# Bit-linear feed-forward: the scale and shift of the second norm computed by VectorE instead of GpSimd

## The chip, the core and the metric

The kernel runs on one core of a Trainium2 chip. Its time is the device time of one execution in microseconds, the median of several runs. Engines are named as the profile names them: PE is TensorE (PEld its weight loads), DVE is VectorE, ACT is ScalarE, POOL is GpSimd, SP is SyncE.

## What is computed

The program is a stack of four attention blocks, each followed by a feed-forward block, over 64 x 64 tokens of width 128 (`x`, kept in SBUF for the whole run). The change touches the first feed-forward block alone, whose reference is:

```python
def layernorm(x, g, b):
    mu = jnp.mean(x, axis=-1, keepdims=True)
    var = jnp.mean((x - mu) ** 2, axis=-1, keepdims=True)
    return (x - mu) * jax.lax.rsqrt(var + LN_EPS) * g + b
def act_quant_fake(x):
    scale = 127.0 / jnp.clip(jnp.max(jnp.abs(x), axis=-1, keepdims=True), 1e-05)
    return jnp.clip(jnp.round(x * scale), -128.0, 127.0) / scale
def bitlinear(x, w, b):
    dqx = act_quant_fake(x)
    dqw = weight_quant_fake(w)
    return jnp.einsum('btd,hd->bth', dqx, dqw) + b
h = layernorm(x, ln1_g, ln1_b)
h = bitlinear(h, w1, b1)                  # 128 -> 512
h = jax.nn.gelu(h, approximate=False)
h = layernorm(h, ln2_g, ln2_b)            # the second norm, over 512
h = bitlinear(h, w2, b2)                  # 512 -> 128
```

`ln2_g` and `ln2_b` are rows of 512 values, the same for every token.

## The kernel before, in words

The 4096 tokens lie as 32 tiles of 128 tokens: partition = token within the tile, free axis = channel. `bit_ffn` (from L905) holds the block. Its first half runs over groups of four tiles and leaves the output of the gelu in `H`, 32 tiles of 128 x 512 float32 in SBUF, and its statistics in `stats`. Then VectorE works out mean, reciprocal deviation and shift of all tokens (L1029 to L1035).

The second half, which the change touches, runs over 16 pairs of tiles. A pair `k` goes through these steps, each on the engine named:

- ACT `normalise` (L1114): writes `(H - mean) * rstd` of the two tiles to slot `k % 4` of `hn` (four slots of 128 x 1024 float32), two ACTIVATE of 128 x 512 (L1117), and raises `n_ready`. It runs two pairs ahead.
- POOL `affine` (L1082): waits for `n_ready`, multiplies the slot by `g2` (L1086), adds `b2n` (L1088), both in place, and raises `affined` after each. `g2` and `b2n` are 128 x 512 tiles that hold the row in every partition; they are read twice through a broadcast access pattern.
- DVE `quantise_h` (L1039): waits for `affined`, then the largest absolute value per token (L1045), its limit and scale (L1046 to L1048, 2 elements per partition each), scaling of either tile (L1049, L1050), and clipping and rounding of both (L1051), which raises `rounded`.
- ACT `to_integers` (L1121) converts to bf16, PE `turn_h` (L1160) transposes eight 128 x 128 blocks, ACT `take_h` (L1126) copies them from PSUM to SBUF, PE `down` (L1167) does the eight matmuls.
- DVE `residual` (L1053): two SCALAR_TENSOR_TENSOR that read PSUM (L1057) and a TENSOR_TENSOR of 128 x 256 that adds to `X` (L1061). DVE `measure_x` (L1063): two BN_STATS for the next block's norm (L1066).

The order on each engine is written out by hand through `pipelined`: a list of (lead, stage), run in that order at each step, unrolled in fours, with a hardware loop in the middle. For VectorE it is

```python
pipelined(dve, PAIRS, [(-2, residual), (0, quantise_h), (-3, measure_x)], period=4)
```

so step `k` is `residual(k - 2)`, `quantise_h(k)`, `measure_x(k - 3)`; ScalarE does `take_h(k - 1)`, `normalise(k + 2)`, `to_integers(k)`. Operations of one engine that depend on each other are joined by `Chain.link` (L62): the instruction raises a semaphore and the engine waits for it. `B_LINKS` is the number of such links in one `quantise_h`. No DMA takes part in this half.

Of the kernel before, what the change touches and what calls it, by code (L numbers as in the profile page):

```python
# [13 lines left out]
ALU = mybir.AluOpType  # L14
# [7 lines left out]
P = 128  # L22
# [56 lines left out]
def wait_past(eng, sem, value):  # L79

    if not isinstance(value, int) or value > 0:
        eng.wait_ge(sem, value)
# [10 lines left out]
def peeled(eng, end, step):  # L93

    step(0, 0, 0)
    step(1, 1, 0)
    in_pairs(eng, 2, end, step)


def pipelined(eng, units, stages, period=2):  # L100

    stages = [(lead, stage, *(more or (0,))) for lead, stage, *more in stages]
    leads = [lead for lead, _, _ in stages]
    first = -(-(period - min(leads)) // period) * period
    end = (units - max(leads)) // period * period  # L110
    def plain(start, stop):
        for s in range(start, stop):
            for lead, stage, beyond in stages:
                if 0 <= s + lead < units + beyond:
                    stage(s + lead, (s + lead) % period, (s + lead) // period)

    if first >= end:
        plain(-max(leads), units - min(leads))
        return
    plain(-max(leads), first)  # L120
    with eng.Fori(0, (end - first) // period) as k:
        for s in range(first, first + period):
            for lead, stage, _ in stages:
                stage(period * k + (s + lead), (s + lead) % period, k + (s + lead) // period)
    plain(end, units - min(leads))
# [776 lines left out]
HID0 = 512  # L902


def bit_ffn(nc, m, t):  # L905
# [5 lines left out]
    with ExitStack() as own:  # L911
        def sb(name, shape, dt=F32):
            return own.enter_context(nc.sbuf_tensor(f"bit_{name}", shape, dt))
# [10 lines left out]
        b1, g2, b2n = sb("b1", [P, HID0]), sb("g2", [P, HID0]), sb("b2n", [P, HID0])  # L924
# [6 lines left out]
        hn = sb("hn", [P, 4, 2, HID0])  # L931
# [5 lines left out]
        def loads(sp):  # L937
# [14 lines left out]
            "xq_ready", "xq_turned", "xqT_ready", "up_ready", "biased", "gelued"))  # L952
        n_ready, hq_ready, hq_turned, hqT_ready, down_ready, x_added = (m.sem(n) for n in (
            "n_ready", "hq_ready", "hq_turned", "hqT_ready", "down_ready", "x_added"))
        affined, rounded, xn_ready, x_affined = m.sem("affined"), m.sem("rounded"), m.sem("xn_ready"), m.sem("x_affined")
        PAIRS = NT // 2
        LOADS = 16 * 8

        with nc.Block() as block:
            @block.vector  # L960
            def _(dve):
# [67 lines left out]
                c = Chain(dve, chained, before + A_LINKS * G)  # L1029
# [4 lines left out]
                c.link(dve.scalar_tensor_tensor(shift2[:, :], mean2[:, :], -1.0, rstd2[:, :], ALU.mult, ALU.mult))  # L1034
                dve.memset(y[:, 0, 0:1], 0.0).then_inc(r_in, 1)  # L1035
                before_b = c.base + c.n
                B_LINKS = 5

                def quantise_h(k, s, n):  # L1039

                    dve.wait_ge(affined, 2 * k + 2)
                    wait_past(dve, rounded, k)
                    c = Chain(dve, chained, before_b + B_LINKS * k)
                    h = hn[:, s, :, :]
                    c.link(dve.tensor_reduce(top2[:, :], h, AX.X, ALU.max, apply_absolute_value=True))  # L1045
                    c.link(dve.tensor_scalar(top2[:, :], top2[:, :], EPS, 1.0 / 127.0, ALU.max, ALU.mult))  # L1046
                    dve.tensor_scalar(undo2[:, s, :], top2[:, :], wmean[:, 1:2], None, ALU.mult)
                    c.link(dve.reciprocal(scale2[:, :], top2[:, :]))  # L1048
                    c.link(dve.tensor_scalar(hn[:, s, 0, :], hn[:, s, 0, :], scale2[:, 0:1], 127.0, ALU.mult, ALU.min))  # L1049
                    c.link(dve.tensor_scalar(hn[:, s, 1, :], hn[:, s, 1, :], scale2[:, 1:2], 127.0, ALU.mult, ALU.min))  # L1050
                    dve.tensor_scalar(h, h, -128.0, MAGIC, ALU.max, ALU.add).then_inc(rounded, 1)  # L1051
# [11 lines left out]
                def measure_x(k, s, n):  # L1063
                    dve.wait_ge(x_added, 2 * k + 2)
                    for j in range(2):
                        dve.bn_stats(m.stats[:, 2 * k + j, :], m.X[:, 2 * k + j, :])  # L1066

                pipelined(dve, PAIRS, [(-2, residual), (0, quantise_h), (-3, measure_x)], period=4)

            @block.gpsimd  # L1070
            def _(pool):
                def affine_x(g, u, n):

                    row = lambda v: v[:, :].unsqueeze(1).broadcast_to([P, 4, D])
                    pool.wait_ge(xn_ready, g + 1)
                    pool.tensor_tensor(xh[:, u, :, :], xh[:, u, :, :], row(g1), ALU.mult).then_inc(x_affined, 1)
                    pool.wait_ge(x_affined, 2 * g + 1)
                    pool.tensor_tensor(xh[:, u, :, :], xh[:, u, :, :], row(b1n), ALU.add).then_inc(x_affined, 1)

                peeled(pool, G, affine_x)  # L1080

                def affine(k, s, n):  # L1082

                    row = lambda v: v[:, :].unsqueeze(1).broadcast_to([P, 2, HID0])
                    pool.wait_ge(n_ready, k + 1)
                    pool.tensor_tensor(hn[:, s, :, :], hn[:, s, :, :], row(g2), ALU.mult).then_inc(affined, 1)  # L1086
                    pool.wait_ge(affined, 2 * k + 1)
                    pool.tensor_tensor(hn[:, s, :, :], hn[:, s, :, :], row(b2n), ALU.add).then_inc(affined, 1)  # L1088

                pipelined(pool, PAIRS, [(0, affine)], period=4)  # L1090

            @block.scalar
            def _(act):
# [1277 lines left out]
def program(nc, t):  # L2371

    with ExitStack() as stack:
        m = Memory(nc, stack)
        load_all(nc, m, t)

        with nc.sbuf_tensor("kept_Oall", [P, NT, D], F32) as Oall:
            attention_diff(nc, m, "at0", "ln0", t["L0_xattn_W_q"], t["L0_xattn_W_k"], t["L0_xattn_W_v"],
                           t["mask_Bx16xSxS2_ff0"], [t["L0_xattn_lambda_" + n] for n in ("q1", "k1", "q2", "k2")], Oall)
            differential_out(nc, m, "do0", Oall, t["L0_xattn_W_o"], t["rms_scale_col"])  # L2380
        m.free_sems()
        bit_ffn(nc, m, t)
        m.free_sems()

        attention_rows(nc, m, "at1", "ln2", *(t["L1_xattn_" + n] for n in ("wq", "wk", "wv", "wo", "bq", "bk", "bv", "bo")),
                  keep_mask=t["mask_1x1xSxS2_ik1"])
        m.free_sems()
        expert_ffn(nc, m, t)
        m.free_sems()

        attention_rows(nc, m, "at2", "ln4", *(t["L2_xattn_" + n] for n in ("WqT", "WkT", "WvT", "WoT", "Wq_b", "Wk_b", "Wv_b", "Wo_b")))
        m.free_sems()
        grouped_ffn(nc, m, t)
        m.free_sems()

        attention_rows(nc, m, "at3", "ln6", *(t["L3_xattn_" + n] for n in ("Wq", "Wk", "Wv", "Wo", "bq", "bk", "bv", "bo")))
        m.free_sems()
        capacity_ffn(nc, m, t)
# [49 lines left out]
```

## Time and profile before

| | |
|---|---|
| three runs | 2232.45, 2234.18, 2238.20 us (median 2234.18) |
| the profiled execution | 2232.57 us, of which the span from first to last instruction 2230.8 us |
| busy in the span | PE 1669.4, DVE 1540.4, POOL 874.6, ACT 825.1 us |
| mean granted TensorE clock | 0.814 |
| second half of this feed-forward | from 448.9 us (first GpSimd instruction) to 583.1 us (last BN_STATS) |

Times in a timeline are from the start of the span. A duration stretches from the start of an instruction to the end of its writes, so that an instruction may start some tens of nanoseconds before the one before it on the same engine is listed as ended. An engine in a wait is not counted as busy, but an instruction that has begun and is held up is: such time looks like work.

### The profile page before, as it was taken

Reading aid. Unit: us, or ns where it says so; the run is one execution under the profiler, and the core shown is the slowest. Engines: PE = TensorE matmul, PEld = TensorE weight load, DVE = VectorE, ACT = ScalarE, POOL = GpSimd, SP = SyncE. Lnnn points to the kernel's source line nnn. Section 1 sums busy time; section 2 is a strip of 40 time slices with the busy share of each in tenths; the row PEclk is TensorE's granted clock in tenths of the full one; section 3 lists DMA queues with packets and bytes.
Section 4 is the critical chain, followed back from the end, with each engine's and each line's share of the span. In section 5 each row is a group of like instructions: output and inputs, shape, how many; then the busy total and the mean of one; then the engine's idle time right before and its main releaser. Section 6 shows DMA issues by size and latency. Waiting matters only on the chain. (4 is left out here: it accounts for less than half of the span.)

```text
span 2230.8 us, 48391 instructions
## 1 busy us (share of the span) xinstructions
PE 1669.4 (75%) x14912; PEld 1187.2 (53%) x14915; DVE 1540.4 (69%) x3682; ACT 825.1 (37%) x1795; POOL 874.6 (39%) x1058
## 2 busy tenths in 40 slices
PE   3999962212499898996898699918999799358993
PEld 2777651011377665664677344417777577335552
DVE  4999976989677753437677899874555687863332
ACT  1544441344355422322564588700000465122221
POOL 1888841266144243005442000005554343027783
PEclk9999976555599889997898899958999799555555
DMA  3222200000000051111001477416774000424446
GB/s 111 68 66 66 65 17 28 0 0 1 7 1 0 16 162 42 40 36 40 1 0 34 151 311 297 198 37 224 282 265 161 7 0 1 120 47 81 81 83 143
DMA packets 178711, 183.56 MB, mean 82 GB/s; under 512 B 101378, under 2 KB 163650, under 8 KB 171202
## 3 DMA queue, kind: packets, MB, share of 16 engines
q1 hardware_dynamic: 154770, 111.88, 16.2%
q10 hardware_dynamic: 9520, 55.94, 7.1%
q0 software_dynamic: 14336, 14.69, 3.6%
q8 instruction: 42, 0.69, 0.1%
q14 instruction: 43, 0.35, 0.1%
HBM read 107.39 MB, written 72.45 MB: 81 GB/s over the span
## 5 line engine op out<-in xcount | busy, mean ns | idle before, releaser
L748 DVE TENSOR_REDUCE at_mx<-at_psS 128x16 f32<-128x1024 f32 x96 | 117.6, 1225 | 93.7 <-PE at_psS L653 93.7
L711 ACT ACTIVATE at_ET<-at_psT 128x512 f32<-128x512 f32 x192 | 114.6, 597 | 172.3 <-PE at_psT L662 171.7
L1922 POOL TENSOR_TENSOR gr_work<-gr_ring 128x512 f32<-128x512 f32 x96 | 121.7, 1280 | 104.3 <-DVE gr_work L1958 97.2
L617 POOL TENSOR_TENSOR at_KM<-at_K,at_mask 128x512 f32<-128x512 f32 x96 | 100.0, 1042 | 154.0 <-ACT at_Q L698 154.0
L2011 PEld LDWEIGHTS gr_psY<-gr_wd,gr_work 128*128 128x128 f32 x1024 | 134.8, 196 | 39.2 <-DVE gr_work L1958 22.8
L388 POOL TENSOR_TENSOR at_E<-at_Z,at_mx 128x512 f32<-128x512 f32 x128 | 130.9, 1044 | 50.1 <-DVE at_mx L513 50.1
L2011 PE MATMUL gr_psY<-gr_wd,gr_work 128*128 128x128 f32 x1024 | 142.4, 283 | 10.7 <-DVE gr_work L1958 10.6
L662 PE MATMUL at_psT<-kept_ident,at_Z 128*128 128x128 f32 x768 | 127.3, 289 | 9.6 <-DVE at_Z L761 4.6
L1844 PE MATMUL gr_psV<-kept_xT,gr_wu 128*128 (+1 forms) x256 | 125.9, 592 | 0.8 <-ACT gr_V L1713 0.8
L249 ACT ACT_TABLE_LOAD x6 | 7.7, 1283 | 314.7 <-PEq L63 299.3
L675 PE MATMUL at_psO<-at_VZ,at_ET 128*64 128x18 f32 x3072 | 106.9, 212 | 15.6 <-ACT at_ET L711 4.2
L675 PEld LDWEIGHTS at_psO<-at_VZ,at_ET 128*64 128x64 f32 x3072 | 97.3, 138 | 34.1 <-ACT at_ET L711 34.1
L2246 POOL DMA_INDIRECT cap_acc<-cap_Y,cap_idx x64 | 102.0, 1593 | 20.8 <-issue 19.6
L1958 DVE TENSOR_TENSOR gr_work<-gr_psF,gr_work 128x512 f32<-128x512 f32 x128 | 85.7, 685 | 35.3 <-PE gr_psY L2011 20.0
L662 PEld LDWEIGHTS at_psT<-kept_ident,at_Z 128*128 128x128 f32 x768 | 81.4, 142 | 53.3 <-issue 37.3
L2285 DVE TENSOR_TENSOR cap_h<-cap_psU,cap_sg 64x128 f32<-64x128 f32 x64 | 18.1, 283 | 119.9 <-ACT cap_sg L2299 119.9
L1923 POOL MEMSET gr_one<- 64x1 f32 x1 | 0.1, 93 | 255.6 <-POOLq L1688 255.6
L2240 POOL DMA_INDIRECT cap_GX<-cap_rows,cap_idx x64 | 63.4, 991 | 91.1 <-DVE cap_idx L2279 76.8
L1844 PE MATMUL gr_psV<-kept_xT,gr_wg 128*128 (+1 forms) x192 | 98.0, 592 | 0.0
L1724 ACT ACTIVATE gr_ring<-gr_psV,gr_bu 128x512 f32<-128x512 f32 x128 | 88.0, 688 | 21.5 <-PE gr_psV L1844 21.5
L763 DVE TENSOR_TENSOR at_Z<-at_psS,at_mx 128x512 f32<-128x512 f32 x128 | 82.5, 686 | 8.6 <-DVE at_mx L748 3.2
L1164 PE MATMUL bit_psT<-kept_identb,bit_hq 128*128 128x128 bf16 x128 | 16.5, 310 | 93.6 <-ACT bit_hq L1124 93.6
(554 smaller groups left out, 4631.9 us busy)
## 6 DMA issues: line engine op xcount, KB each, us to landing
gr_spill<-gr_ring SPq DMA_DIRECT2D x28, 1792.0 KB, 5.7
gr_ring<-gr_spill ACTq DMA_DIRECT2D x28, 1792.0 KB, 7.2
at_amask<-mask_Bx16xSxS_ff SPq DMA_DIRECT2D x128, 128.0 KB, 2.9
cap_acc<-cap_zero SPq DMA_DIRECT2D x2, 2112.0 KB, 12.6
cap_sums<-cap_acc SPq DMA_DIRECT2D x8, 512.0 KB, 7.2
ex_xs<-ex_zero SPq DMA_DIRECT2D x1, 2496.0 KB, 11.1
ex_row<-ex_xs SPq DMA_DIRECT2D x39, 64.0 KB, 1.8
ex_ys<-ex_out SPq DMA_DIRECT2D x39, 64.0 KB, 1.6
```

The costliest lines, as they stand in the source:

```text
L388: pool.tensor_tensor(E[:, a, :].rearrange("p (v k) -> p v k", k=SEQ), Z[:, s % 2, a, :].rearrange("p (v k) -> p v k", k=SEQ), mx[:, s % 2, ...
L617: pool.tensor_tensor(KM[:, s, :, :], K[:, s, :].unsqueeze(1).broadcast_to([P, 4, P]), mask4[:, :].unsqueeze(2).broadcast_to([P, 4, P]), AL ...
L662: last = pe.transpose(psT[:, r * P:r * P + P], Z[:, a, r * P:r * P + P], m.ident[:, :])
L675: last = pe.matmul(psO[rows, t * PW:t * PW + PW], ET[:, 4 * a + r, rows], VZ[:, PAIRS * b + t, :, :].rearrange("p j w -> p (j w)"), start= ...
L711: act.activation(ET[:, 4 * a:4 * a + 4, :].rearrange("p r q -> p (r q)"), psT[:, :], ACT.Exp, scale=QK_SCALE).then_inc(exped, 1)
L748: dve.tensor_reduce(mx[:, :].rearrange("p (g v) -> p g v", v=4), psS[:, :, 0:256].rearrange("p g (v k) -> p g v k", k=SEQ), AX.X, ALU.max) ...
L1724: act.activation(ring[:, u, j % TILES, :], psV[:, j % 4, :], ACT.Silu if is_up else ACT.Identity, bias=bias).then_inc(taken, 1)
L1844: pe.matmul(psV[:, j % 4, :], w, x, start=True, stop=True).then_inc(multiplied, 1)
L1922: pool.tensor_tensor(tp[:, s % 4, :], ring[:, s // 4, first, :], ring[:, s // 4, first + 1, :], ALU.mult).then_inc(pooled, 1)
L1958: dve.tensor_tensor(h[:, s % 2, :], psF[:, s % 4, :], product_of, ALU.mult).then_inc(h_ready, 1)
L2011: last = pe.matmul(psY[:, j, :], h[:, s % 2, j * P:j * P + P], wd[:, s, :], start=False, stop=(s == C - 1), skip_group_check=True)
L2246: pool.indirect_dma_start(accs[s % ACCS], bass.IndirectOffsetOnAxis(ap=idx2[:, s:s + 1], axis=0), Y[:, s % 4, :], None, compute_op=ALU.add ...
```

## The change

The two GpSimd instructions of each pair become two VectorE instructions at the head of `quantise_h`, in place and with the same operands. `quantise_h` waits for ScalarE's `n_ready` instead of `affined`; the semaphore `affined` and GpSimd's loop of this half go. The two are chain links, so `B_LINKS` is 7 instead of 5.

```diff
@@ def quantise_h(k, s, n):
-                B_LINKS = 5
+                B_LINKS = 7
-                    dve.wait_ge(affined, 2 * k + 2)
+                    dve.wait_ge(n_ready, k + 1)
                     wait_past(dve, rounded, k)
                     c = Chain(dve, chained, before_b + B_LINKS * k)
                     h = hn[:, s, :, :]
+                    row = lambda v: v[:, :].unsqueeze(1).broadcast_to([P, 2, HID0])
+                    c.link(dve.tensor_tensor(h, h, row(g2), ALU.mult))
+                    c.link(dve.tensor_tensor(h, h, row(b2n), ALU.add))
                     c.link(dve.tensor_reduce(top2[:, :], h, AX.X, ALU.max, apply_absolute_value=True))
@@ @block.gpsimd
-                def affine(k, s, n):
-
-                    row = lambda v: v[:, :].unsqueeze(1).broadcast_to([P, 2, HID0])
-                    pool.wait_ge(n_ready, k + 1)
-                    pool.tensor_tensor(hn[:, s, :, :], hn[:, s, :, :], row(g2), ALU.mult).then_inc(affined, 1)
-                    pool.wait_ge(affined, 2 * k + 1)
-                    pool.tensor_tensor(hn[:, s, :, :], hn[:, s, :, :], row(b2n), ALU.add).then_inc(affined, 1)
-
-                pipelined(pool, PAIRS, [(0, affine)], period=4)
```

On VectorE, one step `k` in the unrolled head of the second half, before (`bit_top` is `top2`, `bit_b` is `b2`, `kept_X` is `X`):

```order
L1066 BN_STATS kept_stats<-kept_X 128x6 x2
L1057 SCALAR_TENSOR_TENSOR bit_y<-bit_psY,bit_undo,bit_b 128x128 x2
L1061 TENSOR_TENSOR kept_X<-kept_X,bit_y 128x256
L1045 TENSOR_REDUCE bit_top<-bit_hn 128x2
L1046 TENSOR_SCALAR bit_top<-bit_top 128x2
L1047 TENSOR_SCALAR bit_undo<-bit_top,bit_wmean 128x2
L1048 RECIPROCAL bit_scale<-bit_top 128x2
L1049 TENSOR_SCALAR bit_hn<-bit_hn,bit_scale 128x512
L1050 TENSOR_SCALAR bit_hn<-bit_hn,bit_scale 128x512
L1051 TENSOR_SCALAR bit_hn<-bit_hn 128x1024
```

and with the change (the same operations stand three lines further down in the file):

```order
L1069 BN_STATS kept_stats<-kept_X 128x6 x2
L1060 SCALAR_TENSOR_TENSOR bit_y<-bit_psY,bit_undo,bit_b 128x128 x2
L1064 TENSOR_TENSOR kept_X<-kept_X,bit_y 128x256
L1046 TENSOR_TENSOR bit_hn<-bit_hn,bit_g 128x1024
L1047 TENSOR_TENSOR bit_hn<-bit_hn,bit_b2n 128x1024
L1048 TENSOR_REDUCE bit_top<-bit_hn 128x2
L1049 TENSOR_SCALAR bit_top<-bit_top 128x2
L1050 TENSOR_SCALAR bit_undo<-bit_top,bit_wmean 128x2
L1051 RECIPROCAL bit_scale<-bit_top 128x2
L1052 TENSOR_SCALAR bit_hn<-bit_hn,bit_scale 128x512
L1053 TENSOR_SCALAR bit_hn<-bit_hn,bit_scale 128x512
L1054 TENSOR_SCALAR bit_hn<-bit_hn 128x1024
```

Two TENSOR_TENSOR of 128 x 1024 stand between the residual and the reduction; nothing else moved.

On GpSimd, the end of the first half and what follows it, before (the loop over pairs, one of its four steps shown):

```order
L88 COMPARE_AND_BRANCH
L1086 TENSOR_TENSOR bit_hn<-bit_hn,bit_g 128x1024
L1088 TENSOR_TENSOR bit_hn<-bit_hn,bit_b2n 128x1024
...
L121 COMPARE_AND_BRANCH
L959 UNCONDITIONAL_BRANCH
L62 ISA
L598 UNCONDITIONAL_BRANCH
L600 MEMSET at_spare 128x1
```

and with the change:

```order
L88 REGISTER_ALU
L88 COMPARE_AND_BRANCH
L959 UNCONDITIONAL_BRANCH
L62 ISA
L598 UNCONDITIONAL_BRANCH
L600 MEMSET at_spare 128x1
```

GpSimd has nothing to do between the first half and the next attention block.

## Rows read from the trace of the kernel before

**Rows 1.** Windows: us, busy time (x instructions) of PE, PEld, DVE, ACT, POOL; PEclk, DMA share, GB/s.

```profile
453.70:576.90 123.20, 31.01 (x240) 23.13 (x240) 118.02 (x179) 50.64 (x57) 70.74 (x30) 0.50 0.00 0
```

**Rows 2.** Waits from 440 to 600 us: waiter <- releaser: us in total, times, longest.

```profile
POOL bit_hn L1086 <- ACT bit_hn L1117: 65.5, 8, 21.4
ACT bit_hq L1124 <- DVE bit_hn L1051: 57.2, 11, 12.6
...
DVE bit_y L1057 <- PE bit_psY L1172: 3.5, 2, 2.7
```

**Rows 3.** Groups, 440 to 600 us: xcount | busy us, mean ns | idle before.

```profile
L1049 DVE TENSOR_SCALAR bit_hn<-bit_hn,bit_scale 128x512 f32<-128x512 f32 x16 | 22.3, 1392 | 0.6
...
L1047 DVE TENSOR_SCALAR bit_undo<-bit_top,bit_wmean 128x2 f32<-128x2 f32 x16 | 18.3, 1141 | 0.6
...
L1046 DVE TENSOR_SCALAR bit_top<-bit_top 128x2 f32<-128x2 f32 x16 | 9.9, 620 | 0.6
L1050 DVE TENSOR_SCALAR bit_hn<-bit_hn,bit_scale 128x512 f32<-128x512 f32 x16 | 9.7, 608 | 0.6
...
L1061 DVE TENSOR_TENSOR kept_X<-kept_X,bit_y 128x256 f32<-128x256 f32 x8 | 8.2, 1021 | 0.3
L1061 DVE TENSOR_TENSOR kept_X<-kept_X,bit_y 128x256 f32 x8 | 7.9, 982 | 1.2
```

**Rows 4.** Timeline, a pair with GpSimd at work: start, us, engine, line, operation.

```profile
487.34 2.42 POOL L1088 TENSOR_TENSOR bit_hn<-bit_hn,bit_b2n 128x1024 f32<-128x1024 f32 x1
487.46 1.21 DVE L1045 TENSOR_REDUCE bit_top<-bit_hn 128x2 f32<-128x1024 f32 x1
...
488.70 1.08 DVE L1046 TENSOR_SCALAR bit_top<-bit_top 128x2 f32<-128x2 f32 x1
489.72 2.33 POOL L1086 TENSOR_TENSOR bit_hn<-bit_hn,bit_g 128x1024 f32<-128x1024 f32 x1
489.82 2.26 DVE L1047 TENSOR_SCALAR bit_undo<-bit_top,bit_wmean 128x2 f32<-128x2 f32 x1
...
492.18 2.57 DVE L1049 TENSOR_SCALAR bit_hn<-bit_hn,bit_scale 128x512 f32<-128x512 f32 x1
```

**Rows 5.** Timeline of DVE, the pair after another with GpSimd idle.

```profile
512.31 0.59 DVE L1057 SCALAR_TENSOR_TENSOR bit_y<-bit_psY,bit_undo,bit_b 128x128 f32<-128x128 f32 x2
512.93 0.42 DVE L1061 TENSOR_TENSOR kept_X<-kept_X,bit_y 128x256 f32<-128x256 f32 x1
513.28 1.21 DVE L1045 TENSOR_REDUCE bit_top<-bit_hn 128x2 f32<-128x1024 f32 x1
514.52 0.17 DVE L1046 TENSOR_SCALAR bit_top<-bit_top 128x2 f32<-128x2 f32 x1
514.73 0.23 DVE L1047 TENSOR_SCALAR bit_undo<-bit_top,bit_wmean 128x2 f32<-128x2 f32 x1
...
515.06 0.48 DVE L1049 TENSOR_SCALAR bit_hn<-bit_hn,bit_scale 128x512 f32<-128x512 f32 x1
...
517.10 0.59 DVE L1057 SCALAR_TENSOR_TENSOR bit_y<-bit_psY,bit_undo,bit_b 128x128 f32<-128x128 f32 x2
```

**Rows 6.** Timeline: first GpSimd instruction of the half, first and last of DVE's quantising.

```profile
448.92 2.35 POOL L1086 TENSOR_TENSOR bit_hn<-bit_hn,bit_g 128x1024 f32<-128x1024 f32 x1 [21.44 <-ACT bit_hn L1117]
...
453.71 1.22 DVE L1045 TENSOR_REDUCE bit_top<-bit_hn 128x2 f32<-128x1024 f32 x1 [6.43 <-POOL bit_hn L1088]
...
576.14 0.69 DVE L1051 TENSOR_SCALAR bit_hn<-bit_hn 128x1024 f32<-128x1024 f32 x1
```

**Rows 7.** Timeline and groups elsewhere: DVE TENSOR_TENSOR of 1024, DVE instructions of 512 elements.

```profile
2212.15 2.48 DVE L2361 TENSOR_TENSOR kept_X<-kept_X,cap_sums 128x1024 f32<-128x1024 f32 x2 [16.06 <-DMA cap_sums<-cap_acc]
...
L1020 DVE SCALAR_TENSOR_TENSOR bit_H<-bit_psH,bit_undo,bit_b 128x512 f32<-128x512 f32 x32 | 21.7, 742 | 0.0
```

**Rows 8.** Windows in the attention block that follows, and of the last block.

```profile
608.00:610.00 2.00, 0.71 (x5) 0.41 (x5) 1.93 (x4) 1.41 (x3) 0.73 (x1) 0.88 0.00 0
...
2000.00:2231.00 231.00, 178.56 (x544) 114.01 (x544) 77.55 (x388) 56.53 (x185) 160.57 (x123) 0.50 0.49 97
```

More of the change, by code:

```diff
@@ L954, in bit_ffn @@
             "n_ready", "hq_ready", "hq_turned", "hqT_ready", "down_ready", "x_added"))
-        affined, rounded, xn_ready, x_affined = m.sem("affined"), m.sem("rounded"), m.sem("xn_ready"), m.sem("x_affined")
+        rounded, xn_ready, x_affined = m.sem("rounded"), m.sem("xn_ready"), m.sem("x_affined")
         PAIRS = NT // 2
```

## The prediction

> **What bounds the kernel now.** The program runs its blocks one after another, so what the change is worth is read in its own stretch, and I went there first. The windows view of the stretch from VectorE's first to its last quantising instruction [rows 1] shows VectorE busy for 118.0 of 123.2 us, while ScalarE is busy 50.6, GpSimd 70.7 and TensorE 31.0 us, and no DMA moves anything. The waits view [rows 2] says the same from the other side: ScalarE waits 57.2 us for VectorE's rounding, GpSimd waits 65.5 us for ScalarE, which itself waits for VectorE. VectorE waits for TensorE for 3.5 us, of which 2.7 us come at the very end, and for GpSimd once, 6.4 us at the very start [rows 6]. So VectorE sets the end of this stretch, and the work that is to be moved lies beside it, on an engine with time to spare. Read so far, moving it to VectorE should cost.
>
> But is VectorE's busy time work? The groups view [rows 3] has a mean of 1141 ns for L1047, an instruction over 2 elements per partition, and 1392 ns for L1049, while L1050, the same operation on the other tile, takes 608 ns. A mean that mixes two kinds of instances asks for the timeline. In a pair where GpSimd works [rows 4], VectorE's L1047 starts at 489.82, 0.10 us after a GpSimd instruction started at 489.72, and ends at 492.08, as that one ends (492.05). L1046 runs from 488.70 to 489.78, again to the end of a GpSimd instruction (487.34 + 2.42 = 489.76), and L1049 takes 2.57 us from 492.18. In the following pair GpSimd has nothing to do, and the same L1046, L1047 and L1049 take 0.17, 0.23 and 0.48 us [rows 5]. TENSOR_REDUCE takes 1.21 us in both [rows 4, 5], although a GpSimd instruction was running beside it in the first. So some VectorE instructions that only use SBUF (TENSOR_SCALAR, and L1061, whose two inputs both lie there) stand still until the running GpSimd instruction is over, and are listed as busy meanwhile. That is the time the change can win.
>
> **What it removes.** Stretched time per line is the busy time of the 16 instances less 16 undisturbed durations [rows 3, 5]: L1049 22.3 - 16 x 0.48 = 14.6 us; L1047 18.3 - 16 x 0.23 = 14.6; L1046 9.9 - 16 x 0.17 = 7.2; L1050 9.7 - 16 x 0.48 = 2.0; L1061 8.2 + 7.9 - 16 x 0.42 = 9.4. Sum: 47.8 us. With the GpSimd instructions gone I take all of it as gone, since no other instruction of GpSimd runs in this stretch: its next is in the following block. Check by another way: an undisturbed pair lasts from 512.31 to 517.10 [rows 5], 4.8 us, and I allow 4.9 in the hardware loop; 16 pairs at about 4.8 are 76.8 us, and 123.1 us from 453.71 to 576.83 [rows 6] less that is 46.3. The first pairs have no residual and no statistics, so 76.8 is too much and 47.8 the better figure.
>
> The start moves too. GpSimd took up the first pair at 448.92, and VectorE had it at 453.71 [rows 6]. Now VectorE can begin when GpSimd did: 4.8 us won once. The handoff is ScalarE's semaphore in both cases.
>
> **What it adds.** 32 TENSOR_TENSOR of 128 x 1024 float32 with both inputs in SBUF, 16 pairs of one multiplication and one addition. The last block has just this shape on VectorE: two of them, one behind the other with a semaphore in between, take 2.48 us [rows 7]. With 0.03 us to the reduction behind them, as between linked instructions in [rows 5], that is 2.51 us, and 16 x 2.51 = 40.2 us, all of it on the engine that sets the end. Whether reading a 512-wide row twice costs more than reading 1024 elements in line is not to be seen in this row. Bounds: nothing below (it cannot be cheaper than one pass over 1024 elements at the row's rate), and above, two of the dearest VectorE instructions of 512 elements, 2 x 0.742 = 1.484 us [rows 7], which is what a restart at each row would cost; I take the lower end, since it is the row of equal shape and engine. The upper end would add 32 x 0.258 = 8.3 us. Two more links per pair bring register instructions in the loop; in the timeline those between linked instructions hide, so they are set at nothing, and at 0.06 us each as the far end, 8 x 2 x 0.06 = 1.0 us.
>
> **What stays.** The wait on `n_ready` is no new stall: ScalarE normalises two pairs ahead and idles for 57.2 us [rows 2], and its 50.6 us of work over some 15 pairs [rows 1] are 3.4 us a pair beside VectorE's 7.3. `residual(k - 2)` waits for TensorE hardly at all now, and has more VectorE work ahead of it, so not more. Behind the last rounding everything is as before: conversion, transposes, matmuls, last residual, 6.3 us to the end of the stretch. A pair should take 4.8 to 4.9 + 2.5 = 7.3 to 7.4 us, each one the same, where now the 123.1 us over 16 pairs make 7.7, the first ones included.
>
> **The sum**, against the profiled execution: 2232.57 - 47.8 - 4.8 + 40.2 = 2220.2 us. The median of the runs shown is 1.6 us above the profiled execution, so the median should be 2221.8, rounded to **2222.0 us**: 12.2 us or 0.55% less. A measurement of this kernel can tell about 0.3%, 6.7 us, from no change.
>
> **The rivals.**
>
> *VectorE only gets longer* (slower). VectorE is the full engine of this stretch, and what it is given adds to the end; the stretched instructions would stay, because what holds them is VectorE's own traffic with ScalarE on `hn`, and the match with GpSimd's ends a coincidence of a rhythm that all engines share. Price: 2232.57 + 40.2 - 4.8 + 1.6 = 2269.6. It decides if less than 35.4 of the 47.8 us go. For it speaks the windows view at first sight. Against it: ScalarE works in the same way in the pair of [rows 5], where nothing is stretched, and the ends meet GpSimd's within 0.03 us in the two instances of [rows 4] whose partner stands there. The Trainium skill, Perfetto Trace Analysis, section Optimizing Scalar/DVE Operations, says that with a saturated VectorE it may make sense to move work to ScalarE or even GpSimd, which is this rival's case; the next sentence there says that GpSimd and VectorE share an SBUF read port, so that moving work between these two might not help. The trace agrees with that second one (2.26 us where 0.23 are needed). Chance 0.03.
>
> *The new instructions are dear.* Each TENSOR_TENSOR takes up to 1.48 us: 2222.0 + 8.3 + 1.0 = 2231.3, within 0.3%. For it: the broadcast pattern. Against: the price would be an unusual one, and GpSimd's 2.33 to 2.42 us for either instruction [rows 4] tell nothing of VectorE's. Chance 0.05.
>
> *The next block pays it back.* TensorE's granted clock is 0.50 (1.2 GHz) through this stretch and rises to 1.00 (2.4 GHz) at about 608 us, where the 2 us from 608 have a mean of 0.88 [rows 8], some 8 us into the next attention block. In the last block it stays at 0.50 though TensorE is busy for 178.6 of 231 us [rows 8], so a busy TensorE alone does not bring it up. If the block, arriving 12 us earlier, got its clock late, each microsecond at 1.2 GHz would cost at most half a microsecond: 24 us late would eat the gain, and 12 us late would give 2228. For it: the clock moves several times in this kernel. Against: TensorE's work ahead of the rise is the same, only earlier. Chance 0.08, most of it within 0.3%, with about 0.01 of slower.
>
> **How the numbers follow.** The forecast has 0.83: its own range is 2217 to 2227, from the spread of the three runs shown (2232.5 to 2238.2) around a gain of 12, with 1 us for registers. Rivals 0.03, 0.05 and 0.08; 0.01 is left for what I don't see. The likeliest time is 2222.0. The range 2216 to 2229 takes in the forecast's own range and the part of the third rival with a short delay; the dear instructions and the slower rival stay outside. Faster by over 0.3% is the forecast's 0.83 with 0.03 from a short clock delay: 0.86. Within 0.3%: 0.05 and the rest of the clock's, 0.10. Slower: 0.04.
>
> **What would show it.** In the changed profile L1049, L1050 (128 x 2) and L1052 should have one duration each, 0.17, 0.23 and 0.49 us, and L1064 0.43; the two new TENSOR_TENSOR about 1.23 us each; VectorE's first of them at about 448.9; the last rounding ending near 565; GpSimd empty between 447 us and the next block. The next block's clock should rise at about 596. The forecast is wrong if the small instructions are still stretched, if the new ones take over 1.5 us, or if ScalarE's wait for VectorE turns into VectorE's wait for ScalarE.

## The result and the profile after

The changed kernel takes 2221.36 us (median of five runs, 2221.2 to 2224.38), against 2234.18 us before (five runs, 2232.45 to 2238.23). The ratio is 0.9946 with a 95% interval of 0.9933 to 0.9959: 12.8 us or 0.6% faster, clear of the 0.3% that a measurement can tell. The profiled execution took 2221.20 us, its span 2219.4 us. The forecast was 2222.0 us.

The groups view of the changed kernel, 440 to 600 us, has one duration per instruction where the kernel before had mixtures [rows 3]. Columns: instances, busy us, mean ns, idle before.

```profile
L1047 DVE TENSOR_TENSOR bit_hn<-bit_hn,bit_b2n 128x1024 f32<-128x1024 f32 x16 | 19.6, 1225 | 0.5
L1048 DVE TENSOR_REDUCE bit_top<-bit_hn 128x2 f32<-128x1024 f32 x16 | 19.5, 1220 | 0.5
L1046 DVE TENSOR_TENSOR bit_hn<-bit_hn,bit_g 128x1024 f32<-128x1024 f32 x16 | 19.5, 1219 | 1.7 <-ACT bit_hn L1110 1.6
...
L1052 DVE TENSOR_SCALAR bit_hn<-bit_hn,bit_scale 128x512 f32<-128x512 f32 x16 | 7.8, 486 | 0.6
L1053 DVE TENSOR_SCALAR bit_hn<-bit_hn,bit_scale 128x512 f32<-128x512 f32 x16 | 7.8, 486 | 0.6
...
L1050 DVE TENSOR_SCALAR bit_undo<-bit_top,bit_wmean 128x2 f32<-128x2 f32 x16 | 3.6, 228 | 0.6
```

The row to look at is L1050, the same instruction as L1047 before: 3.6 us in all instead of 18.3, though it does what it did. The two new instructions cost 39.1 us of busy time. VectorE's busy time over the whole span nevertheless fell, from 1540.4 to 1532.2 us, and that sum alone would hide that 39 us of work came in and some 48 us of standing still went out.

The start and the end of VectorE's quantising, from the timeline of the changed kernel:

```profile
451.29 1.23 DVE L1046 TENSOR_TENSOR bit_hn<-bit_hn,bit_g 128x1024 f32<-128x1024 f32 x1 [1.58 <-ACT bit_hn L1110]
452.55 1.23 DVE L1047 TENSOR_TENSOR bit_hn<-bit_hn,bit_b2n 128x1024 f32<-128x1024 f32 x1
453.81 1.22 DVE L1048 TENSOR_REDUCE bit_top<-bit_hn 128x2 f32<-128x1024 f32 x1
...
565.33 0.69 DVE L1054 TENSOR_SCALAR bit_hn<-bit_hn 128x1024 f32<-128x1024 f32 x1
...
571.47 0.86 DVE L1069 BATCH_NORM_STATS2 kept_stats<-kept_X 128x6 f32<-128x128 f32 x4
```

From the first scale to the last BN_STATS the half now takes 572.33 - 451.29 = 121.0 us. Before, it took 583.14 - 448.92 = 134.2 us [rows 6, and the table of the profile before]. The half itself gave 13.2 us. This difference is no accident of two executions: the same stretch takes 134.2 us in all three profiles of the kernel before and 121.0 to 121.1 us in both of the changed kernel.

The waits view of the changed kernel, 440 to 600 us (waiter <- releaser: us in total, times, longest), answers [rows 2]:

```profile
ACT bit_hq L1117 <- DVE bit_hn L1054: 44.1, 16, 4.1
...
DVE bit_y L1060 <- PE bit_psY L1165: 2.7, 1, 2.7
...
DVE bit_hn L1046 <- ACT bit_hn L1110: 1.6, 1, 1.6
```

ScalarE still waits for VectorE, 44.1 us instead of 57.2; VectorE is still the engine that sets the end. Its short wait for TensorE ahead of the first residual is gone: 2.7 us in one wait, where it was 3.5 us in two.

### The profile page after: what moved, and what is told of

Its sections match the earlier page's. It is cut to its first block and busy times, and to the rows that moved or that the text cites. A ratio compares the mean times of both kernels' runs of the same rounds, so it can differ in the third digit from the quotient of the medians.

```text
span 2219.4 us, 48378 instructions
## 1 busy us (share of the span) xinstructions
PE 1670.3 (75%) x14912; PEld 1190.7 (54%) x14915; DVE 1532.2 (69%) x3714; ACT 825.5 (37%) x1795; POOL 797.9 (36%) x1026
## 5 line engine op out<-in xcount | busy, mean ns | idle before, releaser
L2004 PEld LDWEIGHTS gr_psY<-gr_wd,gr_work 128*128 128x128 f32 x1024 | 133.2, 194 | 39.1 <-DVE gr_work L1951 23.5
L2278 DVE TENSOR_TENSOR cap_h<-cap_psU,cap_sg 64x128 f32<-64x128 f32 x64 | 18.1, 283 | 120.1 <-ACT cap_sg L2292 120.1
L505 DVE TENSOR_TENSOR at_Z<-at_psS,at_amask 128x512 f32<-128x512 f32 x128 | 81.6, 677 | 8.0 <-PE at_psS L424 7.9
```

The source lines that it names most:

```text
L2004: last = pe.matmul(psY[:, j, :], h[:, s % 2, j * P:j * P + P], wd[:, s, :], start=False, stop=(s == C - 1), skip_group_check=True)
```

## The experiments

Times of single executions scatter by several us in this kernel, since the blocks around the change do. So where a run is read from its trace, I take "the block": from the first instruction of this feed-forward's norm to the first of the next block's norm (L209, `ln1a` to `ln2a`). For the kernel before it is 233.4, 232.1 and 232.9 us in three profiles, for the changed kernel 219.2 in both. "The half" is the stretch measured above, from the first scale (or what stands first in its place) to the last BN_STATS. The diffs are against the changed kernel, and under "Half the change" against the kernel before; they show the main lines, and leave out declarations and counters that follow from them.

### No scale and shift at all: is the stretched time gone by itself?

```diff
-                B_LINKS = 7
+                B_LINKS = 5
-                    c.link(dve.tensor_tensor(h, h, row(g2), ALU.mult))
-                    c.link(dve.tensor_tensor(h, h, row(b2n), ALU.add))
```

> Leaves out the scale and shift of the second norm on every engine (VectorE waits for ScalarE's n_ready; the output lacks g2 and b2n). Theory (GpSimd's instructions held up VectorE's; without them each instruction has its bare duration): no stretched instruction, VectorE's pair 4.8 to 4.9 us, the changed kernel's 2221 less 32 x 1.26 = 40 us, so about 2181; ScalarE's own round (1.15 + 1.1 + 1.0 + 1.5 = 4.8 us) then comes close to VectorE's and may add a few us. Rival (the stretch is the price of VectorE and ScalarE passing hn to each other quickly, and is hidden in the changed kernel because the two new instructions give ScalarE time): L1045 to L1050 durations go up again towards 1 us, time above 2200.

Measured: 2184.62 us in one run, the block 181.2 us. From its groups view:

```profile
L1049 DVE TENSOR_SCALAR bit_hn<-bit_hn,bit_scale 128x512 f32<-128x512 f32 x16 | 7.8, 487 | 0.6
...
L1047 DVE TENSOR_SCALAR bit_undo<-bit_top,bit_wmean 128x2 f32<-128x2 f32 x16 | 3.7, 228 | 0.6
```

No instruction is stretched, so the quick exchange of `hn` between VectorE and ScalarE is not what stretches. The half takes 82.1 us, 38.9 less than in the changed kernel, where the two instructions taken out make 40.3: 0.8 us of the rest is VectorE's wait for TensorE ahead of the first residual, which is back (3.5 us in two waits); 0.6 us I can't assign. ScalarE now waits for VectorE's rounding for only 5.1 us, so it comes close to VectorE's pace, but VectorE does not wait for it after the first pair.

### GpSimd works beside, on a tile of its own

GpSimd does its two old instructions per pair on a tile `aside` that nobody reads, and nobody waits for it. This is extra work, with no effect on the output.

```diff
+                def beside(k, s, n):
+                    pool.wait_ge(n_ready, k + 1)
+                    row = lambda v: v[:, :].unsqueeze(1).broadcast_to([P, 2, HID0])
+                    pool.wait_ge(aside_done, 2 * k + 1)
+                    pool.tensor_tensor(aside[:, :, :], aside[:, :, :], row(g2), ALU.mult).then_inc(aside_done, 1)
+                    pool.wait_ge(aside_done, 2 * k + 2)
+                    pool.tensor_tensor(aside[:, :, :], aside[:, :, :], row(b2n), ALU.add).then_inc(aside_done, 1)
```

> The changed kernel, with GpSimd doing its old two TENSOR_TENSOR per pair on a tile of its own that nobody reads (extra work, nobody waits for it). Theory (a running GpSimd instruction holds up any VectorE instruction with two SBUF streams, whatever the data): the small TENSOR_SCALAR instances reach 2.3 us again, the new TENSOR_TENSOR of VectorE are held too, 40 to 60 us more than the changed kernel: 2262 to 2282. Rival (the stretch came from both engines working on the same tile hn, or from the handoff between them): nothing is stretched, 2221.

Measured: 2285.45 us in one run, the block 282.9 us, 63.7 us more than in the changed kernel. That is above the expected range, and the rival (2221) is out. The timeline of this run shows the hold in both directions:

```profile
451.29 1.23 DVE L1047 TENSOR_TENSOR bit_hn<-bit_hn,bit_g 128x1024 f32<-128x1024 f32 x1 [1.58 <-ACT bit_hn L1122]
451.34 3.38 POOL L1091 TENSOR_TENSOR bit_aside<-bit_aside,bit_g 128x1024 f32<-128x1024 f32 x1 [20.55 <-ACT bit_hn L1122]
452.56 3.25 DVE L1048 TENSOR_TENSOR bit_hn<-bit_hn,bit_b2n 128x1024 f32<-128x1024 f32 x1
454.80 3.21 POOL L1093 TENSOR_TENSOR bit_aside<-bit_aside,bit_b2n 128x1024 f32<-128x1024 f32 x1
...
515.86 2.34 POOL L1091 TENSOR_TENSOR bit_aside<-bit_aside,bit_g 128x1024 f32<-128x1024 f32 x1 [6.76 <-ACT bit_hn L1122]
516.01 2.22 DVE L1050 TENSOR_SCALAR bit_top<-bit_top 128x2 f32<-128x2 f32 x1
518.26 2.38 DVE L1051 TENSOR_SCALAR bit_undo<-bit_top,bit_wmean 128x2 f32<-128x2 f32 x1
518.28 2.34 POOL L1093 TENSOR_TENSOR bit_aside<-bit_aside,bit_b2n 128x1024 f32<-128x1024 f32 x1
```

At 451.29 VectorE is first. GpSimd's instruction, 0.05 us behind it, takes 3.38 instead of 2.34 us, longer by about the time until VectorE's ends (452.52). Then VectorE's next one is behind and is held until GpSimd's ends at 454.72, and takes 3.25 instead of 1.23. In these rows whoever begins first runs at its full pace and the other stands still; they don't share. Later (the rows from 515.86 on) both GpSimd instructions of a pair fall on the two 2-element TENSOR_SCALAR, which take 2.22 and 2.38 us instead of 0.17 and 0.23, so a pair loses 4.2 of the 4.7 us that GpSimd works. In the kernel before, 47.8 us were lost over 16 pairs, 3.0 us each; that the handoff through `affined` made the engines meet in this other way is my reading, not shown. How much is lost depends on where the instructions fall, which is what my range had not allowed for.

### GpSimd only writes

The same with two MEMSET of 128 x 1024 per pair on `aside`, which read nothing. Extra work as before.

```diff
+                for k in range(PAIRS):
+                    pool.wait_ge(n_ready, k + 1)
+                    for i in range(2 * k, 2 * k + 2):
+                        wait_past(pool, aside_done, i)
+                        pool.memset(aside[:, :, :], 0.0).then_inc(aside_done, 1)
```

> The changed kernel, with GpSimd doing two MEMSET of 128x1024 per pair on a tile of its own (it writes SBUF and reads nothing). Theory A (any running GpSimd instruction holds VectorE): per pair about two of VectorE's instructions are held for part of 0.9 us, 10 to 25 us more: 2231 to 2246. Theory B (only a GpSimd instruction that reads holds a TENSOR_TENSOR, while TENSOR_SCALAR is held by one that writes too): the new TENSOR_TENSOR keep 1.22 us, only L1049, L1050, L1052 to L1054 get longer: 2221 to 2236. Theory C (reading alone matters): 2221.

Measured: 2234.71 us in one run, the block 237.3 us, 18.1 us more than in the changed kernel (the half 17.5 us more). The time lies within the bands of A and of B, so single rows have to tell. The timeline of its first pair and of the pair at 500 us:

```profile
447.50 1.23 DVE L1047 TENSOR_TENSOR bit_hn<-bit_hn,bit_g 128x1024 f32<-128x1024 f32 x1 [1.59 <-ACT bit_hn L1116]
447.53 6.12 POOL L1089 MEMSET bit_aside<- 128x1024 f32 x6 [21.41 <-ACT bit_hn L1116]
448.76 1.23 DVE L1048 TENSOR_TENSOR bit_hn<-bit_hn,bit_b2n 128x1024 f32<-128x1024 f32 x1
...
501.14 1.96 POOL L1089 MEMSET bit_aside<- 128x1024 f32 x2 [6.59 <-ACT bit_hn L1116]
501.39 0.72 DVE L1050 TENSOR_SCALAR bit_top<-bit_top 128x2 f32<-128x2 f32 x1
502.15 0.97 DVE L1051 TENSOR_SCALAR bit_undo<-bit_top,bit_wmean 128x2 f32<-128x2 f32 x1
502.28 0.84 DVE L1052 RECIPROCAL bit_scale<-bit_top 128x2 f32<-128x2 f32 x1
```

This is theory B, but for one instruction that it did not name. Two TENSOR_TENSOR with both inputs in SBUF ran at their 1.23 us with MEMSETs beside them all the way, where in the run before a TENSOR_TENSOR of GpSimd held the second up to 3.25 us. TENSOR_SCALAR is held by a MEMSET too: the five of a pair are longer by 18.3 us over the 16 pairs, against the 17.5 by which the half grew. RECIPROCAL is listed with a mean of 705 instead of 157 ns; it starts 0.13 us behind the held L1051 and ends with it, so its 8.8 us lie inside those of L1051. Whether the MEMSET holds it, or only the instruction ahead of it does, no run here tells. The Trainium skill, SBUF — State Buffer, section Who interferes with whom, says just this: a VectorE instruction with two SBUF inputs contends with a GpSimd instruction that reads SBUF and not with one that only writes it, while one in a two-port mode, which TENSOR_SCALAR can enter, contends with either, and the second to start blocks until the first is done. The trace agrees on all three points (1.23 beside MEMSET, 3.25 beside TENSOR_TENSOR, 0.97 instead of 0.23 for TENSOR_SCALAR beside MEMSET). That these TENSOR_SCALAR run in a two-port mode is not shown here; the trace has only their durations.

### Half the change

GpSimd keeps the multiplication, VectorE takes the addition.

```diff
+                    c.link(dve.tensor_tensor(h, h, row(b2n), ALU.add))
@@ gpsimd, affine
-                    pool.wait_ge(affined, 2 * k + 1)
-                    pool.tensor_tensor(hn[:, s, :, :], hn[:, s, :, :], row(b2n), ALU.add).then_inc(affined, 1)
```

> Half the change: GpSimd keeps the multiplication, VectorE does the addition. Theory: stretches follow GpSimd's instructions, so with 16 instead of 32 of them about half of 47.8 us is left (24), VectorE gets 16 x 1.26 = 20 us, and starts 2.4 us later than in the changed kernel: 2221 - 20 + 24 + 2 = 2227, between 2219 and 2234. Rival (each GpSimd instruction can hold one VectorE instruction for its whole 2.35 us, 37 us): 2240.

Measured: 2231.02 us (median of ten, 2224.58 to 2235.51) against 2234.85 us before on the same chip, ratio 0.9984 (0.9969 to 1.0). Within the expected band, below the rival's 2240, and no gain that can be told. Its groups view:

```profile
L1052 DVE TENSOR_SCALAR bit_hn<-bit_hn,bit_scale 128x512 f32<-128x512 f32 x16 | 28.3, 1766 | 0.6
L1046 DVE TENSOR_TENSOR bit_hn<-bit_hn,bit_b2n 128x1024 f32<-128x1024 f32 x16 | 21.6, 1352 | 4.1 <-POOL bit_hn L1088 4.0
...
L1053 DVE TENSOR_SCALAR bit_hn<-bit_hn 128x1024 f32<-128x1024 f32 x16 | 13.1, 820 | 0.6
```

Most of the hold now falls on one instruction, L1052: 28.3 instead of 7.8 us, 20.5 us more. With the 2.0 of L1046, 2.0 of L1053 and 4.4 of two others, 28.9 us are lost under 16 GpSimd instructions, 1.8 us each, where 32 of them cost 47.8. Half of GpSimd's instructions left 60% of the loss, and the 20 us of added work ate what was won. The half of the block takes 132.3 us, 1.9 less than before, where the whole change took 13.2 off.

### The same move in the first half

GpSimd also scales and shifts in the first half of this block (`affine_x`). Here that goes to VectorE too.

```diff
-                A_LINKS = 5
+                A_LINKS = 7
-                    dve.wait_ge(x_affined, 2 * g + 2)
+                    dve.wait_ge(xn_ready, g + 1)
+                    c.link(dve.tensor_tensor(x, x, row(g1), ALU.mult))
+                    c.link(dve.tensor_tensor(x, x, row(b1n), ALU.add))
```

> The changed kernel, with the scale and shift of the FIRST norm (GpSimd's affine_x, two TENSOR_TENSOR of 128x512 per group of four tiles, 8 groups) moved to VectorE too. Theory (what pays is the end of held-up instructions, and there are none in that half: GpSimd's two instructions lie beside SCALAR_TENSOR_TENSOR that read PSUM and BN_STATS, 741 and 676 ns each with and without GpSimd beside them): VectorE, busy throughout there, gets 16 x 0.72 = 11.5 us more and starts its first group about 2.6 us earlier: 9 us slower than the changed kernel, about 2230. Rival (VectorE is simply the better place for such work whenever it and GpSimd are both in use): no slower than the changed kernel, 2221 or less.

Measured: 2226.76 us (median of six) against 2221.92 us for the changed kernel on the same chip and 2237.32 us before (ratio to before 0.995, 0.9937 to 0.9963); the block 225.5 against 219.2 us, 6.3 us longer, all of it ahead of the second half, which takes its 121.1 us. The medians are 4.8 us apart. The rival is out: the same move, on the same engines, costs 6.3 us here, where it gained 13.2 there. The 9 us that I expected were too many. The groups view of this run, and, for L1005, of the changed kernel, whose wait for GpSimd is what is saved:

```profile
L1007 DVE TENSOR_TENSOR bit_xh<-bit_xh,bit_b1n 128x512 f32<-128x512 f32 x8 | 5.5, 692 | 0.3
...
L1006 DVE TENSOR_TENSOR bit_xh<-bit_xh,bit_g 128x512 f32<-128x512 f32 x8 | 5.4, 680 | 0.1
```

```profile
L1020 DVE SCALAR_TENSOR_TENSOR bit_H<-bit_psH,bit_undo,bit_b 128x512 f32<-128x512 f32 x32 | 21.7, 741 | 0.0
L1026 DVE BATCH_NORM_STATS2 bit_stats<-bit_H 128x6 f32<-128x512 f32 x32 | 19.6, 676 | 0.0
...
L1005 DVE TENSOR_REDUCE bit_amax<-bit_xh 128x4 f32<-128x512 f32 x8 | 5.4, 674 | 5.7 <-POOL bit_xh L1081 5.7
```

The two instructions add 16 x 0.72 = 11.5 us, and the end of VectorE's waits for GpSimd saves 5.7 us (I had put 2.6 for it, one pair of GpSimd's instructions, when the row says 5.7, in three waits of the first groups): 5.8 us, 6.3 measured. In that half GpSimd's work lies beside SCALAR_TENSOR_TENSOR that read one input from PSUM (741 ns) and BN_STATS (676 ns), and neither is held: with GpSimd gone from that half they take 742 and 678 ns.

### A version that is faster than both

VectorE is the full engine and ScalarE waits 44 us for it. So ScalarE takes over the scaling to integers: two ACTIVATE per pair compute `hn * scale + 1.5 x 2^23`, which rounds, in place of VectorE's L1052 to L1054. The limits of 127 and -128 are left out.

```diff
-                    c.link(dve.reciprocal(scale2[:, :], top2[:, :]))
-                    c.link(dve.tensor_scalar(hn[:, s, 0, :], hn[:, s, 0, :], scale2[:, 0:1], 127.0, ALU.mult, ALU.min))
-                    c.link(dve.tensor_scalar(hn[:, s, 1, :], hn[:, s, 1, :], scale2[:, 1:2], 127.0, ALU.mult, ALU.min))
-                    dve.tensor_scalar(h, h, -128.0, MAGIC, ALU.max, ALU.add).then_inc(rounded, 1)
+                    dve.reciprocal(scale2[:, s, :], top2[:, :]).then_inc(rounded, 1)
@@ scalar, to_integers
                     act.wait_ge(rounded, k + 1)
+                    for j in range(2):
+                        last = act.activation(hn[:, s, j, :], hn[:, s, j, :], ACT.Identity, bias=minus[:, 1:2], scale=scale2[:, s, j:j + 1])
+                    last.then_inc(scaled, 1)
+                    act.wait_ge(scaled, k + 1)
@@
-                pipelined(act, PAIRS, [(-1, take_h), (2, normalise), (0, to_integers)], period=4)
+                pipelined(act, PAIRS, [(2, normalise), (-1, take_h), (0, to_integers)], period=4)
```

> The changed kernel, with VectorE's L1052 to L1054 (scaling of either tile, clipping and rounding) taken over by ScalarE as two ACTIVATE per pair (times scale plus 1.5 x 2^23; the limits of +-127 and -128 are left out, since scaling by 127 over the largest absolute value keeps within them), and ScalarE's order changed to normalise, take_h, to_integers. Theory (VectorE's own work sets the pair): VectorE's pair 7.4 - 1.65 = 5.7 us, ScalarE's 1.5 + 1.0 + 1.6 + 0.2 + 1.15 = 5.5 us, so 16 x 1.65 = 26 us less and about 2 us more at the end: 2197, up to 2205 if ScalarE becomes the limit. Rival (another wait takes over at the old pair time): above 2212.

Measured: 2195.64 us (median of four, 2194.09 to 2198.63) against 2221.92 for the changed kernel on the same chip, and 2237.32 before: ratio to before 0.9815 (0.9798 to 0.9831). 26 us less than the changed kernel, and close to the expected 2197. Only 22.1 us of them lie in the half, which takes 98.9 instead of 121.0 us: the moved instructions took 1.65 us a pair, 26.4 us, and VectorE now waits for TensorE for 4.9 us more than in the changed kernel. The other 4 us of the medians' difference are outside the half, in parts that the edit does not touch, and I can't assign them. The waits view of this run:

```profile
ACT bit_hn L1115 <- DVE bit_scale L1052: 13.3, 14, 1.5
...
DVE bit_y L1058 <- PE bit_psY L1167: 7.6, 8, 3.9
```

ScalarE's wait for VectorE is down to 13.3 us and VectorE has begun to wait for TensorE's result, 7.6 us instead of 2.7: the two engines are nearly balanced at 5.8 to 5.9 us a pair.

The order alone, as a control:

```diff
-                pipelined(act, PAIRS, [(-1, take_h), (2, normalise), (0, to_integers)], period=4)
+                pipelined(act, PAIRS, [(2, normalise), (-1, take_h), (0, to_integers)], period=4)
```

> The changed kernel with ScalarE's order alone changed to normalise, take_h, to_integers, as in the run act_scales. Theory: VectorE sets the pair, so the second half lasts as long as in the changed kernel (121 us from the first scale to the last BN_STATS), time 2218 to 2226. If ScalarE's order mattered, the half would be over 1 us shorter or longer.

Measured: 2219.66 us in one run; the half takes 121.1 us, as in the changed kernel. The order gains nothing by itself; what `act_scales` gains in the half is the moved work's.

### The clock of the next block

In the changed kernel the granted clock rises at 604.9 us, not at about 596, as I had forecast. The next block, from its norm to the norm after it, takes 189.1 us instead of 186.3. The third rival seemed to have come true in part, so I looked whether it comes with the change.

> The changed kernel once more, on the same chip as the others of this call. Theory (the clock's rise in the next attention block scatters between some 24 and 31 us after that block's norm begins, whatever the change, and each microsecond costs about 0.4 us of that block): time 2219 to 2226, the block from its norm to the next norm between 186 and 190 us according to the rise. Rival (the change itself makes the rise late, by its denser or earlier work): the rise is at 31 us again and the block takes 189 us again.

> The kernel before, profiled again. So far the granted clock rises 24.4 us after the next block's norm begins in the kernel before and in mult_pool, and after 28.8 to 31.7 us in the eight others, the changed kernel twice at 31.6 to 31.7; the block takes 186.3 and 188 to 189 us. Theory (scatter): this profile may lie anywhere between 24 and 32 us, and 186 to 189 us. Rival (the change causes the late rise; GpSimd-bound rhythm gives the early one): 24.4 us and 186.3 us again.

> The same as before_again, once more: theory (scatter) anywhere between 24 and 32 us; rival (cause in the kernel) 24.4 us and 186.3 us, and then all three profiles of the kernel before agree.

> The changed kernel with one MEMSET of 128x4096 on VectorE (about 4.3 us) at the end of the second half, so that the next block begins 4.3 us later and TensorE's work is the same in order and rhythm. Theory (scatter, or a phase against time that the program does not set): the rise anywhere between 24 and 32 us after the norm begins. Rival (the work of the half decides): 31.6 us again, 189 us for the block. Time 2221 + 4.3, give or take 3.

> As delay4, with 128x8192 (about 8.5 us). Theory: the rise anywhere between 24 and 32 us. Rival: 31.6 us and 189 us. Time 2221 + 8.5, give or take 3.

The two delays add one MEMSET to VectorE at the end of the half (`dve.memset(H[:, 0:8, :], 0.0)` and `H[:, 0:16, :]`). Measured:

| profile | rise of the clock, us after the block's norm begins | the block that follows, us |
|---|---|---|
| before | 24.4 | 186.3 |
| before_again | 29.0 | 188.0 |
| before_third | 31.6 | 188.5 |
| changed | 31.7 | 189.1 |
| after_again | 31.6 | 188.6 |
| delay4 | 30.1 | 188.2 |
| delay8 | 29.8 | 188.1 |
| mult_pool | 24.4 | 186.4 |
| act_scales | 30.2 | 188.2 |

The five other profiles (`none`, `beside_tt`, `beside_ms`, `first_too`, `act_order`) lie between 28.8 and 31.1 us, with 187.9 to 188.4 us for the block that follows. The kernel before alone covers nearly the whole spread, from 24.4 to 31.6 us. The windows that tell it (length, busy times of PE, PEld, DVE, ACT and POOL, then the granted clock, DMA share and GB/s), first of the profile before, then of before_third, whose block begins at 582.7:

```profile
607.00:608.00 1.00, 1.00 (x11) 0.69 (x4) 0.51 (x1) 0.00 (x0) 0.00 (x0) 0.50 0.00 0
608.00:609.00 1.00, 0.53 (x3) 0.23 (x2) 0.95 (x2) 0.43 (x2) 0.00 (x0) 0.75 0.00 0
609.00:610.00 1.00, 0.18 (x2) 0.18 (x3) 0.98 (x2) 0.98 (x2) 0.73 (x1) 1.00 0.00 0
```

```profile
613.00:614.00 1.00, 1.00 (x6) 0.97 (x5) 0.93 (x2) 0.55 (x1) 0.00 (x0) 0.50 0.00 0
614.00:615.00 1.00, 1.00 (x30) 0.81 (x28) 1.00 (x2) 0.67 (x3) 0.00 (x0) 0.87 0.00 0
615.00:616.00 1.00, 1.00 (x19) 0.97 (x16) 0.92 (x3) 0.06 (x1) 1.00 (x1) 1.00 0.00 0
```

So a late rise needs no change, and the 2.8 us that the next block seems to have paid back are mostly a matter of which execution was profiled: against the two other profiles of the kernel before, the changed kernel's next block is longer by 0.1 to 1.1 us. The rival, as a price of 2.8 us, falls. The early rise came in two of the four profiles in which GpSimd hands pairs to VectorE and in none of the other ten; that the change makes a late rise more frequent is therefore neither shown nor excluded. What sets the moment stays open. after_again and the changed kernel agree to 0.1 us, which no run here explains, and the delays went with a rise 1.5 and 1.8 us earlier in the block, which is within the scatter. The delays' times were 2226.30 and 2226.93 us (expected 2225.3 and 2229.5), the blocks 224.1 and 228.3 us, 4.9 and 9.1 us longer. Of this 4.3 and 8.5 us are the delay (the MEMSET itself takes 3.47 and 6.88 us), and 0.6 us lie ahead of the second half, which takes 121.0 us in both.

## Why the prediction was right, point by point

**What bounds the stretch.** Right: VectorE, whose busy time was partly standing still. `none` takes the added work away and shows no stretch, `beside_tt` gives GpSimd work on data of its own and brings it back.

**What it removes.** Forecast 47.8 us plus 4.8 for the start. From the first reduction to the end of the last rounding VectorE took 123.1 us; now, from the first multiplication, 566.02 - 451.29 = 114.7, of which 16 x 2.52 = 40.3 are new, so 74.4 are left and 48.7 went. Of the 0.9 us above the forecast, 0.8 is the short wait for TensorE ahead of the first residual (3.5 us in two waits before, 2.7 in one now). I had written that this wait does not grow; it went. The start came as forecast: VectorE waits 1.6 us for its first pair, where it waited 6.4. The times that I gave for it on the clock of the profile missed (448.9 for the first new instruction, 565 for the last rounding's end, against 451.29 and 566.02), mostly since in this execution the block itself began 3.3 us later (354.0 against 350.7).

**What it adds.** Forecast 2.51 us a pair, measured 2.52 (451.29 to 453.81), 40.3 us instead of 40.2. The last block's pair of TENSOR_TENSOR [rows 7] was the right row, and reading a row twice through a broadcast costs nothing that can be seen: the instances take 1216 to 1226 ns, where that pair took 2.48 us for two. The two links per pair in the loop cost nothing that can be seen.

**The sum.** 12.4 us were forecast for the half, 13.2 came: too small by the 0.8 us of that wait. The whole time agrees to 0.6 us (2222.0 against 2221.36), which is partly luck. Between the two profiled executions (2232.57 and 2221.20 us) 11.4 us went: 13.2 in the half and 1.0 ahead of it in the same block, while the next block gave back 2.8; what came ahead of this block was 3.3 us longer and what came after the next one 3.3 us shorter, which cancels by chance. On another chip the medians differ by 15.4 us (ratio 0.993, 0.9913 to 0.9947, that is 12 to 19 us), an interval that holds the 13.2 of the half too. The parts outside the half hold nothing that the change touches, and I can't assign their differences.

**The rivals.** "VectorE only gets longer" would have given 2269.6. It fell with the first row of the new profile, and its mechanism with `none`. It describes the first half rightly, though, where the same move costs 6.3 us. "The new instructions are dear" fell: 1.22, not 1.48 us. "The next block pays it back" fell as far as the three profiles of the kernel before can tell, while its price was about right: a rise 7.3 us later goes with a block 2.8 us longer, 0.4 us for each, below the bound of a half. My forecast of where the clock would rise (596) was wrong by 9 us: 7.3 of them because I took one profile's moment for a property of the kernel.

## What to carry to other kernels

Work on GpSimd beside a full VectorE was free in this kernel only where it met VectorE instructions that are not held, here TENSOR_REDUCE, BN_STATS and those with a PSUM input; beside TENSOR_SCALAR and, when GpSimd reads, TENSOR_TENSOR on SBUF it stopped VectorE. Ask for every GpSimd instruction which VectorE instructions it will meet. If a group's mean is several times that of a like instruction, look at single instances: the time of the hold is listed as busy, and the busy share of the held engine then says nothing on whether it can take more work. And take a difference of a few us from a part's own stretch over several profiles, not from two whole executions: here the half agreed within 0.05 us between profiles of one kernel, the block around it within 1.3 us and the whole execution only within several us.

## What was not expected

- A hold costs up to nearly the whole of the other engine's instruction whatever the size of the held one: 2.38 us on an instruction over 2 elements that takes 0.23 alone, beside one of 2.34. For its size, a small TENSOR_SCALAR on the way to a result thus loses most.
- The loss depends on where the instructions fall: 3.0 us a pair in the kernel before, 4.0 in `beside_tt` (63.7 over 16) with the same GpSimd instructions.
- The same program on the same engine order saw its clock rise 24.4, 29.0 and 31.6 us into the next block in three executions.
